# A Mamba-style mixer and a top-2 expert layer on one core: two small copies change engine, a weight split is cut into pieces, loops get hinted branches

## The reference

```python
h = layernorm(x) * (1 + ca) + sa
x = x + ga * mamba(h)                 # projection, conv of 4 taps, scan over time, gate, projection
h = layernorm(x) * (1 + cb) + sb
out = swiglu(h, shared)               # 2 x 938 hidden units
cw = normalised top-2 of softmax(h @ gate.T) over 8 experts
for e in range(8):
    out = out + cw[..., e:e+1] * swiglu(h, expert[e])
x = x + gb * out
```

## Time and profile before

| | us |
|---|---|
| median of 3 runs | 966.2 |
| lowest and highest run | 965.87, 968.27 |
| span of the profiled execution | 967.3 |

### The profile page before, as it was taken

How to read it: one execution, slowest core, us unless ns; L and a number is a source line. 1 busy time by engine, 2 the same in 40 slices (tenths; PEclk the granted TensorE clock), 3 DMA queues, 4 the chain that set the end, 5 groups by cost and what they waited for, 6 DMA issues and landing times.

```text
span 967.3 us, 11710 instructions
## 1 busy us (share of the span) xinstructions
PE 740.5 (77%) x3134; PEld 555.3 (57%) x3135; DVE 678.6 (70%) x1358; ACT 430.4 (44%) x721; POOL 395.5 (41%) x299
## 2 busy tenths in 40 slices
PE   4556988879787888887766969696995977869940
PEld 1435756657565555565554747474874866657830
DVE  3576878787877879774637676767658677676637
ACT  2324564646465564732432525252542543435520
POOL 2231434535445444443325352626225344342136
PEclk9566798979898989978977979797997997979985
DMA  8210000000000001010322020201102102000017
GB/s 250 29 60 17 15 9 25 20 22 22 22 22 22 22 0 38 6 42 6 114 82 71 28 75 24 78 22 39 66 20 71 33 14 79 23 20 25 25 56 224
DMA packets 38204, 44.40 MB, mean 46 GB/s; under 512 B 5334, under 2 KB 28880, under 8 KB 38184
## 3 DMA queue, kind: packets, MB, share of 16 engines
q1 hardware_dynamic: 33576, 35.69, 12.1%
q0 software_dynamic: 4608, 8.47, 2.7%
HBM read 31.42 MB, written 13.76 MB: 47 GB/s over the span
## 4 chain that ended last, share of the span: by engine, by line
PE 48%; DVE 25%; issue 14%; POOL 5%; ACT 3%; DMA 2%; DVEq 0%; SPq 0%; ACTq 0%; POOLq 0%
PE PS L554 45%; DVE aux_w L1468 5%; PE PS L557 3%; DVE acc L1121 2%; DVE nx_a L1092 2%; DVE prod L1100 2%; POOL al L409 2%; DVE al L1105 2%; POOL sorted_dram L443 1%; POOL c_exp L424 1%; POOL rstd_b L418 1%; DVE yT L1205 1%; DVE nx_b L1092 1%; ACT xsT L915 1%; DMA stage<-result_dram 1%
## 5 line engine op out<-in xcount | busy, mean ns | idle before, releaser
L1100 DVE TENSOR_TENSOR prod<-PS,sg 128x512 f32<-128x512 f32 x216 | 149.0, 690 | 145.8 <-PE PS L554 130.3
L884 ACT CAST ah<-prod 128x512 fp32r<-128x512 f32 x216 | 132.9, 615 | 204.1 <-DVE prod L1100 204.1
L554 PE MATMUL PS<-xh,w_lo 128*128 128x512 f32 x432 | 188.2, 436 | 29.2 <-DVE prod L1100 17.0
L513 POOL DMA_INDIRECT result_dram<-y_rows,aux_d x80 | 91.3, 1142 | 272.4 <-DVE y_rows L1451 238.1
L879 ACT ACTIVATE sg<-PS 128x512 f32<-128x512 f32 x216 | 129.2, 598 | 154.8 <-PE PS L554 154.4
L554 PE MATMUL PS<-xh,w_hi 128*128 128x512 f32 x432 | 177.8, 412 | 0.0
L554 PE MATMUL PS<-xl,w_hi 128*128 128x512 f32 x432 | 177.8, 411 | 0.0
L1105 DVE TENSOR_TENSOR al<-prod,ah 128x512 fp32r<-128x512 f32 x188 | 162.7, 865 | 12.1 <-ACT ah L884 10.3
L554 PE MATMUL PS<-al,w_hi 128*128 128x512 f32 x216 | 96.8, 448 | 74.4 <-DVE al L1105 67.5
L554 PEld LDWEIGHTS PS<-xh,w_lo 128*128 128x128 f32 x432 | 87.6, 203 | 60.8 <-DVE prod L1100 25.2
L443 POOL DMA_INDIRECT sorted_dram<-h,slot x64 | 69.9, 1092 | 101.6 <-DVE slot L1291 73.1
(11 more groups left out here) (215 smaller groups left out, 1120.2 us busy)
## 6 DMA issues: line engine op xcount, KB each, us to landing
stage<-in_w_gu SPq DMA_DIRECT2D x18, 469.0 KB
xin<-sorted_dram SPq DMA_DIRECT2D x20, 260.0 KB, 2.7
stage<-in_w_dn SPq DMA_DIRECT2D x9, 448.0 KB
tab<-mods_dram SPq DMA_DIRECT2D x8, 384.0 KB, 3.4
sorted_dram<-pad SPq DMA_DIRECT2D x8, 260.0 KB, 2.6
out<-X SPq DMA_DIRECT2D x4, 512.0 KB, 3.2
stage<-result_dram SPq DMA_DIRECT2D x3, 512.0 KB, 5.2
result_dram<-y_rows,aux_d POOLq DMA_INDIRECT x80, 2.3
```

What stands on the lines that cost most here:

```text
L513: pool.indirect_dma_start(out=result_dram, out_offset=bass.IndirectOffsetOnAxis(ap=aux_d[:, 0, r:r + 1].bitcast(U32), axis=0), in_=y_rows[ ...
L554: return nc.tensor.matmul(out, lhsT, rhs, start=start, stop=stop, **k)
L884: A.copy(ah[:, c % 3, :], prod[:, c % 3, :]).then_inc(s["ah_ready"], 1)
L1100: V.tensor_tensor(prod[:, c % 3, :], bank("up", where, c), sg[:, c % 3, :], ALU.mult).then_inc(s["prod_done"], 1)
```

## The change

- `take_tile` on DVE no longer copies the two columns. On ACT `split_tile` copies both at once to a new buffer aux_next (after the high part xh), and a new `move_aux`, after high(6), waits for the landed rows and copies to aux_w and to aux_d. `give_rows` waits for it.
- Destinations travel as float32 numbers until `move_aux` makes them int32.
- `split_expert` takes the place of `split_hi` and `split_lo` for the experts 1 to 7: 6 pieces of 512 columns, high and low in turn, the low part one piece behind.
- All `Fori` loops are made with `hint_back_edge=True` and an explicit engine: every iteration begins with an instruction that names the branch that closes the loop.

```diff
+        def loop(engine, first, end):
+            return nc.Fori(first, end, engines=[engine.engine], hint_back_edge=True)
+        PIECES = 6
...
+            def split_expert(x, buf):
+                pool.wait_ge(s["raw_in"], 16 * NRAW * (x + 1))
+                apart(pool)
+                n = WC // PIECES
+                for k in range(PIECES + 1):
+                    if k < PIECES:
+                        at = slice(k * n, (k + 1) * n)
+                        V.tensor_tensor(w_hi[buf][:, at], stage[:, at], M["ones"][:, 0:1].to_broadcast([P, n]),
+                                        ALU.mult).then_inc(s["cut_hi"], 1)
+                    if k:
+                        at = slice((k - 1) * n, k * n)
+                        pool.wait_ge(s["cut_hi"], PIECES * (x - 2) + k)
+                        last = V.tensor_tensor(w_lo[buf][:, at], stage[:, at], w_hi[buf][:, at].bitcast(F32),
+                                               ALU.subtract)
+                last.then_inc(s["split_done"], 1)
...
                     pool.wait_ge(s["y_bank_done"], SHARED + first)
-                    split_hi(e + 2, 1 - buf)
-                    split_lo(e + 2, 1 - buf)
-                with pool.Fori(0, tiles) as t:
+                    split_expert(e + 2, 1 - buf)
+                with loop(pool, 0, tiles) as t:
...
             def split_tile(i):
                 act.wait_ge(s["xt_done"], i + 1)
                 A.copy(xh[:], PS[:, 7, :]).then_inc(s["rh_ready"], 1)
+                act.wait_ge(s["aux_moved"], i + 1)
+                A.copy(aux_next[:], xin[:, :, P:P + 2]).then_inc(s["aux_read"], 1)
+
+            def move_aux(i):
+                act.wait_ge(s["results_out"], 64 * (i + 1))
+                act.wait_ge(s["aux_read"], i + 2)
+                A.copy(aux_w[:], aux_next[:, :, 0])
+                A.copy(aux_d[:], aux_next[:, :, 1]).then_inc(s["aux_moved"], 1)
...
                         high(SHARED + i, c)
+                        if c == FC - 2:
+                            move_aux(i)
...
-            def take_tile(i, moved):
+            def take_tile(i):
                 dve.wait_ge(s["rh_ready"], i + 1)
                 V.tensor_tensor(xl[:], PS[:, 7, :], xh[:].bitcast(F32), ALU.subtract).then_inc(s["rl_ready"], 1)
-                if moved:
-                    dve.wait_ge(s["aux_moved"], i)
-                V.tensor_copy(aux_w[:, 1, :], xin[:, :, P])
-                V.tensor_copy(aux_d[:, 1, :], xin[:, :, P + 1].bitcast(I32)).then_inc(s["aux_read"], 1)
...
                 dve.wait_ge(s["yt_done"], SHARED + 1 + i)
+                dve.wait_ge(s["aux_moved"], i + 1)
...
-                        if c == FC - 3:
-                            dve.wait_ge(s["results_out"], 64 * (i + 1))
-                            dve.wait_ge(s["aux_read"], i + 2)
-                            V.tensor_copy(aux_w[:, 0, :], aux_w[:, 1, :])
-                            V.tensor_copy(aux_d[:, 0, :], aux_d[:, 1, :]).then_inc(s["aux_moved"], 1)
```

More of the change, by code:

```diff
@@ L95, in constants @@
     return (np.ascontiguousarray(big, np.float32), np.ascontiguousarray(small, np.float32),
-            np.ascontiguousarray(token, np.int32))
+            np.ascontiguousarray(token, np.float32))
 SMALL = {}
@@ L127, in adaln_block @@
         S = {n: small[:, o:o + k] for n, (o, k) in SMALL.items()}
-        token2 = sb("token2", [P, CH, 2], I32)
+        token2 = sb("token2", [P, CH, 2])
         w_in = sb("w_in", [P, 4, P])
@@ L215, in adaln_block @@
         y_rows = sb("y_rows", [P, TR, P])
-        aux_w = sb("aux_w", [P, 2, TR])
-        aux_d = sb("aux_d", [P, 2, TR], I32)
+        aux_next = sb("aux_next", [P, TR, 2])
+        aux_w = sb("aux_w", [P, TR])
+        aux_d = sb("aux_d", [P, TR], I32)
         fin = [stage[:, k * GC * 2 * P:(k + 1) * GC * 2 * P] for k in range(3)]
@@ L242, in adaln_block @@
             xh_ready xl_ready logits_done lg_ready soft_in soft_out picked_ready counts_done counts_read
-            rows_ready sorted_out dve_chain raw_in split_hi split_done piece_hi piece_done gate_done up_done silu_done prod_done
+            rows_ready sorted_out dve_chain raw_in split_hi split_done cut_hi piece_hi piece_done gate_done up_done silu_done prod_done
             ah_ready al_ready al_late y_bank_done y_sb_ready yt_done y_out gated_free tile_in xt_done rh_ready
@@ L326, in _ @@
             load_raw(1)
-            with sp.Fori(1, G) as g:
+            with loop(sp, 1, G) as g:
                 sp.wait_ge(s["tab_free"], g)
@@ L353, in expert @@
                     load_raw(e + 2)
-                with sp.Fori(0, tiles) as t:
+                with loop(sp, 0, tiles) as t:
                     load_tile(e * REGION + t * TILE, first + t)
                 return first + tiles
-            with sp.Fori(0, E - 1) as e:
+            with loop(sp, 0, E - 1) as e:
                 expert(e, True)
@@ L458, in _ @@
             pool.wait_ge(s["setup_mem"], 1)
-            V.memset(pad[:, :, P + 1:P + 2].bitcast(I32), NOWHERE).then_inc(s["setup_mem"], 1)
+            V.memset(pad[:, :, P + 1:P + 2], float(NOWHERE)).then_inc(s["setup_mem"], 1)
             pool.wait_ge(s["setup_mem"], 2)
@@ L491, in _ @@
             body(1, True, True, False)
-            with pool.Fori(2, G - 1) as g:
+            with loop(pool, 2, G - 1) as g:
                 body(g, True, True, True)
@@ L500, in _ @@
             apart(pool)
-            pool.sem_inc(s["split_hi"], 1)
             pool.sem_inc(s["split_done"], 1)
@@ L514, in results @@
                         out=result_dram, out_offset=bass.IndirectOffsetOnAxis(
-                            ap=aux_d[:, 0, r:r + 1].bitcast(U32), axis=0),
+                            ap=aux_d[:, r:r + 1].bitcast(U32), axis=0),
                         in_=y_rows[:, r, :], in_offset=None, bounds_check=2 * TOKENS - 1,
@@ L524, in expert @@
                     pool.wait_ge(s["y_bank_done"], SHARED + first)
-                    split_hi(e + 2, 1 - buf)
-                    split_lo(e + 2, 1 - buf)
-                with pool.Fori(0, tiles) as t:
+                    split_expert(e + 2, 1 - buf)
+                with loop(pool, 0, tiles) as t:
                     results(first + t + 1)
             results(0)
-            with pool.Fori(0, E // 2 - 1) as k:
+            with loop(pool, 0, E // 2 - 1) as k:
                 expert(2 * k, 1, True)
@@ L804, in _ @@
             body(1, True, True, False)
-            with pe.Fori(2, G - 1) as g:
+            with loop(pe, 2, G - 1) as g:
                 body(g, True, True, True)
@@ L860, in expert @@
                 apart(pe)
-                with pe.Fori(0, tiles) as t:
+                with loop(pe, 0, tiles) as t:
                     tile_body(buf, first + t)
                 return first + tiles
-            with pe.Fori(0, E // 2 - 1) as k:
+            with loop(pe, 0, E // 2 - 1) as k:
                 expert(2 * k + 1, 0, expert(2 * k, 1))
@@ L1022, in _ @@
             body(1, True, True, False, False)
-            with act.Fori(2, G - 1) as g:
+            with loop(act, 2, G - 1) as g:
                 body(g, True, True, True, False)
@@ L1042, in split_tile @@
                 A.copy(xh[:], PS[:, 7, :]).then_inc(s["rh_ready"], 1)
+                act.wait_ge(s["aux_moved"], i + 1)
[5 more added lines that the diff above has]
+                A.copy(aux_d[:], aux_next[:, :, 1]).then_inc(s["aux_moved"], 1)
             split_tile(0)
-            with act.Fori(0, E) as e:
+            with loop(act, 0, E) as e:
                 tiles, first = tiles_of(act, e)
-                with act.Fori(0, tiles) as t:
+                with loop(act, 0, tiles) as t:
                     i = first + t
@@ L1285, in place @@
                     V.tensor_tensor(h2[:, k, :, P], top[:, 4 + k, :], top[:, 7, :], ALU.mult)
-                    V.tensor_copy(h2[:, k, :, P + 1].bitcast(I32),
+                    V.tensor_copy(h2[:, k, :, P + 1],
                                   token2[:, bass.ds(g * GC, GC), k:k + 1].rearrange("p j o -> p (j o)"))
@@ L1333, in _ @@
             V.memset(aux_w[:], 0.0)
-            link(V.memset(aux_d[:], NOWHERE))
+            V.memset(aux_d[:], NOWHERE).then_inc(s["aux_moved"], 1)
             dve.wait_ge(s["setup_mem"], 2)
@@ L1398, in _ @@
             before = chain["n"]
-            with dve.Fori(2, G - 1) as g:
+            with loop(dve, 2, G - 1) as g:
                 chain["base"], chain["n"] = (g - 2) * PER_BODY + before, 0
@@ L1434, in _ @@
             gate_shared(g, WIDE)
-            def take_tile(i, moved):
+            def take_tile(i):
                 dve.wait_ge(s["rh_ready"], i + 1)
                 V.tensor_tensor(xl[:], PS[:, 7, :], xh[:].bitcast(F32), ALU.subtract).then_inc(s["rl_ready"], 1)
-                if moved:
-                    dve.wait_ge(s["aux_moved"], i)
-                V.tensor_copy(aux_w[:, 1, :], xin[:, :, P])
-                V.tensor_copy(aux_d[:, 1, :], xin[:, :, P + 1].bitcast(I32)).then_inc(s["aux_read"], 1)
```

(10 more changed lines are left out.)

## The result

The changed kernel takes 980.3 us (median of 4 runs, 979.7 to 983.0), the kernel before 967.2 (965.9 to 968.3): ratio 1.0147, 95% interval 1.0124 to 1.017. It is 13 us slower. Its profiled execution has a span of 978.3 us, against 967.3.

A forecast was written before the change was run, and what follows sets the result against it. Bound by PE's matmuls plus DVE ops held behind POOL's long split ops, 12.3 us for each of 7 splits. 966 - 86 (holds) + 31.5 (late rows and xin) + 14 (lower clock) = 926, rounded to 927 us; range 900 to 950.

The forecast's parts named there:

- What bounds the kernel: PE matmuls, with DVE's al and copy held behind POOL's long split ops, then TensorE back at half clock, at 7 splits.
- 86: Us lost to the 7 splits before the change, 12.3 each, after taking issue gaps and slow start from 97.3.
- That DVE gets its turn between two POOL ops is seen twice: Split on POOL: al slips in between pieces, so it waits at most 1.3 us.
- The second sighting: Four nx_a ops beside four POOL ops of about 1.2 us took 0.3 to 1.3 us, one for each.
- rival D: Pieces on POOL don't let DVE in; al held for 14 us against 12.3 now: 978 us; chance 0.03.
- The later steps: After the stall goes: split length S, late result rows and xin, restart at lower clock, copies and hints.
- S: Length of POOL's split in 12 pieces: 14.0 us plus 2.9 for about 8 al ops, 17 us; bounds 14 and 24.5.
- the sum: Forecast time: 966 - 86 + 31.5 (lateness) + 14 (lower clock) = 926 us, rounded to 927; 0.36 per al entered S.
- Rows late by 3.8 to 6, xin by 4.6: Behind each split ACT waits for rows, PE for xin (two-tile experts); side by side, 4.5 us taken for each of 7.
- The 19 tiles: Stage two, first xh cast to last: about 397 us after the change, against 436.6 before.
- The copies on ACT: Moving DVE's copies alone would move the wait to the next al; their leaving the tile's end gives nothing.
- Hints: Loop ends: no instructions fetched, so nothing to save; taken at 0, bounds 3 us lost or 9.7 gained.

## Why the prediction was wrong, step by step

**What bounds the kernel** was right: each split cost a hold and a restart of TensorE at the lower clock. With gaps and half the split early the 19 tiles take 845.0 - 486.9 = 358.1 us (first and last xh cast of that run), 78.5 less than before, where I had put 86 as the most to be had. The xh casts of that kernel:

```profile
L1063 ACT CAST xh<-PS x20: 577/579/585, 486.9 to 845.0; 128x512 fp32r<-128x512 f32 x20
```

**The step that failed** is "That DVE gets its turn between two POOL ops is seen twice". Both sightings were true, and neither was of the boundary that counts. In the first, between w_hi and w_lo of the kernel before stands a wait for the end of w_hi, and the rows show it as a gap of 0.08 us. The changed kernel's order, with the low part one piece behind, is there to make just such waits end early, so that pieces queue without a gap. The diff says so plainly: `cut_hi` is waited for after the next high piece has been given. The second sighting was of queued ops in part. It was also read wrongly: the four nx_a stand beside three POOL ops, a pair op, w_hi and w_lo (151.42 to 155.17); the first got in at the queued boundary behind the pair op, the next two at the gap between w_hi and w_lo, one of them without waiting (0.335 us). A queued boundary can let DVE in, as the kernel with one gap in each pair shows again; the one at the start of the changed kernel's split does not, whatever the form of the DVE op. So the 12 pieces are, for al, one op of 13.3 us in place of two of 5.33 and 7.01: longer than the two together, and without the handover in their middle.

My rival D had this case at 0.03 and priced it at 978; the measured time is 980.3. The mechanism is D's; that the price came so close is partly luck. D took 14 us of pieces against 12.3; they last 13.3 against 12.4, which by D's own sum gives 0.9 for each split, or 972. The 19 tiles lost 2.1 for each split, and some 3 us of the time are those of the hints, which D left out. I had named the 0.08 us gap as the evidence against D and had not asked whether the change keeps it.

**The later steps** were sized for a split that lets al in, and the run with gaps tests them:

- S: 17 forecast, 17.2 measured. In expert 1 seven al get in, not eight, each for 0.33 us against 0.36 in the sum, and the gaps, which the sum did not have, make up for the difference. The Trainium skill's page "SBUF — State Buffer" (Who interferes with whom) would have POOL pay the whole 0.61, as an exclusive lock. The measurement says 0.33 behind a gap of 0.07 and 0.45 where there is no gap (1.49 against 1.04, one gap in each pair): less than the whole either way.
- Rows late by 3.8 to 6, xin by 4.6: ACT waited 5.0 us, PE 4.4 in expert 1. Over the seven splits ACT waited 31.6 us, where the sum has 31.5.
- The 19 tiles: 397 forecast, 397.1 measured. The time: 927 forecast for the change, 929.9 measured for the change with gaps.
- The copies on ACT: right that alone they would only move the wait to the next al. I gave them nothing; they are worth 6.5 us beside the two long ops and nothing beside the pieces.
- Hints: taken at 0 with 3 as the upper bound; 3.9, 2.9 and 9.4 us in three pairs of kernels, the 2.9 with intervals that overlap. That they save nothing was right. Part of the loss can be seen. PE's gap at an expert change is 2.35 us in the kernel after and 2.11 before; in the pair with half the split early it is 2.36 against 2.13 us. The chain of the kernel with hints:

```profile
571.41 2.36 issue
...
763.33 1.73 issue
765.07 4.60 PE PS L579 x12
```

The chain of the one without, at the same expert changes:

```profile
563.30 2.13 issue
...
754.12 1.67 issue
755.79 3.03 PE PS L575 x12
```

Behind the last of these changes the same 12 matmuls take 4.60 us with hints and 3.03 without: the granted clock in these stretches is 0.63 and 1.00 of full speed. So such a gap is sometimes followed by a spell at 1.2 GHz and sometimes not. That this adds up to all of the 9.4 was not shown.

## What to carry to other kernels

Cutting a long GpSimd op in pieces can give VectorE nothing: queued in the order of this change, 12 pieces held it as one op. With each low piece right behind its own high piece, which it waits for, VectorE got in at every boundary at which it waited, and 980 became 926 to 930 us. Waits at the other boundaries gained nothing. Whether an order lets the other engine in is seen in the duration of its longest op in the trace. When a trace shows that one engine slips in between two ops of another, look at what made the gap, and ask whether the change keeps it. And behind a stall that goes look for what it covered: here two transfers, whose lateness could be worked out from the rows of before to within a microsecond in expert 1. It was then taken away by using POOL's idle time.

## What the runs showed of the hardware that was not expected

- Twelve POOL ops of 1.04 and 1.26 us, queued back to back and begun by two high pieces, hold a DVE op that reads and writes SBUF alone for 13.4 to 14.2 us, also one with a single input and one of 128 columns. An increment of a semaphore ahead of every piece does not end the hold.
- Queued POOL ops do not always hold DVE. al got in at 20 of 20 queued boundaries from a low to a high piece in the two kernels with one gap in each pair, at a price of 0.45 us for POOL. In stage one of the kernel before a pair op runs from 203.49 to 204.77, the next begins at 204.73, and nx_a, handed over at 204.20, ends between them, at 204.85. What makes the difference was not found.
- A hinted back edge cost 3.9 and 9.4 us in two pairs of kernels of 885 to 970 us, and 2.9 in a third whose intervals overlap, with about 30 iterations on each engine. In the kernel before no instructions were fetched from 171 to 399 us, so there was little to save.
